# The attention out-projection as three fp16 products of high and low parts, in place of one fp32 product

## What is computed

```
x = queries                                    # (4, 1024, 128) fp32
q, k, v = split(layernorm(x) @ [Wq, Wkv])      # 16 heads of 64; q, k rotated in 32 of them
attn = softmax(q @ k.T * 64 ** -0.5)
out  = (attn @ v) of all heads side by side    # (4, 1024, 1024)
x = x + out @ Wout + bout                      # <- the out-projection; Wout is (1024, 128)
x = x + gelu(layernorm(x) @ U1 @ V1 + b1) @ U2 @ V2 + b2
```

## Time and profile before

| | |
|---|---|
| median of 3 runs | 1453.45 us (1453.07 to 1453.85) |
| the profiled execution's own time | 1453.33 us |
| its span, first to last instruction | 1451.5 us |
| granted TensorE clock, mean | 0.986 of full speed |
| PE busy | 1386.7 us (96%) |
| DVE busy | 1161.0 us (80%) |
| POOL busy | 989.8 us (68%) |
| ACT busy | 789.7 us (54%) |
| PE's 504 records of the out-projection in TILE | 66.7 us |

### The profile page before, as it was taken

The page is one execution under the profiler, slowest core; times in us unless marked ns, Lnnn a source line. Parts: engine busy times, 40 slices in busy tenths (PEclk is TensorE's granted clock), DMA queues, the critical chain, the costliest instruction groups (busy, mean ns, idle before and its releaser), DMA issues.

```text
span 1451.5 us, 25538 instructions
## 1 busy us (share of the span) xinstructions
PE 1386.7 (96%) x7313; PEld 518.3 (36%) x7313; DVE 1161.0 (80%) x1296; ACT 789.7 (54%) x1511; POOL 989.8 (68%) x499
## 2 busy tenths in 40 slices
PE   3698999999999999999999999999999999999897
PEld 1133333343434333333433333343433333343334
DVE  6786888888788888878888888878888887889644
ACT  3254555555555555646555555555555564655456
POOL 4379776858486677858677685848667784867831
PEclk9699999999999999999999999999999999999999
DMA  5402121220313122130312222031312213031002
GB/s 160 87 20 63 37 66 38 58 58 15 83 34 80 22 59 58 39 78 15 80 37 62 40 58 58 15 81 36 80 22 58 58 37 79 15 80 28 11 16 58
DMA packets 69553, 75.46 MB, mean 52 GB/s; under 512 B 26804, under 2 KB 36536, under 8 KB 69272
## 3 DMA queue, kind: packets, MB, share of 16 engines
q1 hardware_dynamic: 68080, 74.14, 22.8%
q10 hardware_dynamic: 1448, 1.00, 0.3%
HBM read 22.04 MB, written 2.35 MB: 17 GB/s over the span
## 4 chain that ended last, share of the span: by engine, by line
PE 48%; issue 23%; POOL 22%; DVE 4%; ACT 2%; POOLq 1%; DMA 0%; ACTq 0%; SPq 0%; DVEq 0%
PE O L389 17%; PE S L377 9%; POOL SA L677 9%; PE S L378 8%; PE M L398 5%; POOL T L653 5%; PE TILE L307 3%; PE TILE L331 3%; POOL STAGE L664 3%; POOL YR L656 2%; DVE MX L603 2%; ACT PF L512 1%; PE TILE L323 1%; PE TILE L313 1%; POOL WRAW L293 1%
## 5 line engine op out<-in xcount | busy, mean ns | idle before, releaser
L677 POOL TENSOR_TENSOR SA<-PF 128x1024 f32<-128x1024 f32 x254 | 658.7, 2601 | 364.8 <-DVE SUM L610 303.0
L512 ACT ACTIVATE PF<-S 128x512 f32<-128x512 f32 x1024 | 555.8, 596 | 456.7 <-PE S L378 455.1
L603 DVE TENSOR_REDUCE MX<-M 128x1 f32<-128x1024 f32 x508 | 597.3, 1217 | 179.4 <-PE M L398 179.2
L389 PE MATMUL O<-PF,V 128*64 128x512 f32 x2048 | 497.9, 607 | 0.0
L377 PE MATMUL S<-QK 128*128 128x512 f16 x1024 | 393.2, 384 | 4.6 <-ACT PF L512 3.2
L378 PE MATMUL S<-QK 128*128 128x512 f16 x1024 | 389.1, 380 | 0.0
L613 DVE TENSOR_TENSOR SUM<-SUM,SA 128x1024 f32<-128x1024 f32 x126 | 225.2, 1787 | 5.3 <-POOL SA L677 4.2
L389 PEld LDWEIGHTS O<-PF,V 128*64 128x64 f32 x2048 | 124.8, 136 | 249.9 <-issue 179.4
L377 PEld LDWEIGHTS S<-QK 128*128 128x128 f16 x1024 | 99.2, 97 | 250.7 <-ACT PF L512 107.9
L398 PE MATMUL M<-QK 64*128 64x512 f16 x1016 | 169.2, 410 | 16.2 <-DVE MX L603 8.5
L398 PEld LDWEIGHTS M<-QK 64*128 64x128 f16 x1016 | 53.2, 152 | 222.6 <-issue 210.1
(11 more groups left out here) (107 smaller groups left out, 750.6 us busy)
## 6 DMA issues: line engine op xcount, KB each, us to landing
QK<-STAGE SPq DMA_DIRECT2D x128, 256.0 KB, 3.9
QK<-STAGE SPq DMA_DIRECT2D x128, 128.0 KB, 3.1
RB<-den SPq DMA_DIRECT2D x124, 128.0 KB, 3.0
X<-in_L_attn_queries SPq DMA_DIRECT2D x4, 512.0 KB, 13.1
out<-X SPq DMA_DIRECT2D x8, 256.0 KB, 2.3
RT<-DS SPq DMA_DIRECT2D x124, 2.0 KB, 1.7
WRAW<-in_L_attn_Wkv SPq DMA_DIRECT2D x1, 1024.0 KB, 9.0
ROPE<-in_rope SPq DMA_DIRECT2D x1, 1024.0 KB, 12.3
```

The lines of the kernel that those rows point to most:

```text
L389: mm = e.matmul(O[DH * z:DH * z + DH, :], V[:, h, kt * DH:(kt + 1) * DH], PF[:, t % SLOTS, z * HALF:(z + 1) * HALF], start=(kt == 0), stop ...
L512: e.activation(PF[:, t % SLOTS, z * HALF:(z + 1) * HALF], S[:, z * HALF:(z + 1) * HALF], ACT.Exp, scale=EXP_SCALE).then_inc(exped, 1)
L603: e.tensor_reduce(MX[:, place % 2, q:q + 1], bank, AX, ALU.max).then_inc(max_read, 1)
L677: e.tensor_tensor(SA[:, (t // 2) % 2, :], PF[:, t % SLOTS, :], PF[:, t % SLOTS + 1, :], ALU.add).then_inc(two_summed, 1)
```

## The change

The product `OS @ WO` in fp32 becomes `OH @ WH + OL @ WH + OH @ WL` in fp16, accumulated in one PSUM group. `WH` is Wout times 16 rounded to fp16 and `WL` what is left; both are made once, ahead of the loop, by ACT and DVE from a raw copy of Wout that is now loaded into the last slot of `PF`. For each pair, `OH` is `OS` rounded to fp16, copied by ACT behind its work of steps 16 and 26 (`HIGH_AT`), and `OL` is `OS - OH`, made by DVE in steps 17 and 27 (`LOW_AT`). The residual add divides by 16. `OH` and `OL` have one buffer each, so ACT's copy waits until the pair before has been added.

```diff
+HIGH_AT = {16: 1, 26: 0}
+LOW_AT = {17: 1, 27: 0}
...
-        WO = sb("WO", [P, HEADS // 2, D], F32)
+        WO = sb("WO", [P, 2, HEADS // 2, D], F16)
...
+        OH = sb("OH", [P, 2, HALF], F16)
+        OL = sb("OL", [P, 2, HALF], F16)
...
+        WO_RAW = PF[:, SLOTS - 1, :].rearrange("p (c n) -> p c n", n=D)
...
         def out_tile(e, q, parity, pair, z, bank):
-            e.wait_ge(normed, q + 1)
+            e.wait_ge(out_lo, q + 1)
             for j in range(4):
-                mm = e.matmul(bank[:, j * P:(j + 1) * P], OS[:, parity, z, j * P:(j + 1) * P], WO[:, pair, :],
-                              start=True, stop=True)
+                tokens = slice(j * P, (j + 1) * P)
+                for n, (o, w) in enumerate(((OH, 0), (OL, 0), (OH, 1))):
+                    mm = e.matmul(bank[:, tokens], o[:, z, tokens], WO[:, w, pair, :], start=(n == 0), stop=(n == 2))
             mm.then_inc(tile_made, 1)
...
+        def act_out_high(e, q, parity):
+            e.wait_ge(normed, q + 1)
+            wait(e, added, 2 * q)
+            e.activation(OH[:, :, :], OS[:, parity, :, :], ACT.Copy).then_inc(out_hi, 1)
...
             act_tiles(e, it, t)
+            if t in HIGH_AT and not (it.first and HIGH_AT[t]):
+                act_out_high(e, it.pair(HIGH_AT[t]), HIGH_AT[t])
...
-            e.tensor_tensor(xs, bank.rearrange("p (t d) -> p t d", d=D), xs, ALU.add).then_inc(added, 1)
+            e.scalar_tensor_tensor(xs, bank.rearrange("p (t d) -> p t d", d=D), 1.0 / WSCALE, xs, ALU.mult,
+                                   ALU.add).then_inc(added, 1)
...
+        def dve_out_low(e, q, parity):
+            e.wait_ge(out_hi, q + 1)
+            e.tensor_tensor(OL[:, :, :], OS[:, parity, :, :], OH[:, :, :], ALU.subtract).then_inc(out_lo, 1)
...
             if it.last:
                 dve_last(e, t)
+            if t in LOW_AT and not (it.first and LOW_AT[t]):
+                dve_out_low(e, it.pair(LOW_AT[t]), LOW_AT[t])
...
+            act.wait_ge(wo_in, 16)
+            act.activation(WO[:, 0, :, :], WO_RAW, ACT.Copy, scale=WSCALE).then_inc(wo_hi, 1)
             act_max(act, 0, 0)
...
             for c in range(EARLY - 1):
+                if c == 1:
+                    act_out_high(act, PAIRS - 1, 1)
                 gelu(c + 1)
                 q_copy(c)
...
+            dve.wait_ge(wo_hi, 1)
+            dve.scalar_tensor_tensor(WO[:, 1, :, :], WO_RAW, WSCALE, WO[:, 0, :, :], ALU.mult,
+                                     ALU.subtract).then_inc(wo_lo, 1)
...
             norm.then_inc(normed, 1)
+            dve_out_low(dve, PAIRS - 1, 1)
```

More of the change, by code:

```diff
@@ L204, in build @@
         inverse_spread, stored = sem("inverse_spread"), sem("stored")
+        wo_hi, wo_lo, out_hi, out_lo = (sem(n) for n in ("wo_hi", "wo_lo", "out_hi", "out_lo"))
         powers_set = sem("powers_set")
@@ L777, in _ @@
                 sp.dma_start(X[:, b * KT:(b + 1) * KT, :], xr[:, b * KT:(b + 1) * KT, :]).then_inc(x_in[b], 16)
-            sp.dma_start(WO[:, :, :], wout_d.rearrange("(c p) n -> p c n", p=P)).then_inc(wo_in, 16)
+            sp.dma_start(WO_RAW, wout_d.rearrange("(c p) n -> p c n", p=P)).then_inc(wo_in, 16)
             sp.wait_ge(rot_lo, 4)
@@ L930, in body @@
                     if it.first and OUT_AT.get(t) == (0, 0):
-                        e.wait_ge(wo_in, 16)
+                        e.wait_ge(wo_lo, 1)
                     pe_step(e, it, t)
```

## The result

The changed kernel took 1459.09 us (median of 6 runs, 1456.73 to 1460.14), the kernel before 1452.79 (6 runs, 1452.22 to 1453.85): a ratio of 1.0040, 95% interval 1.0027 to 1.0053. So it is slower, by about 6 us, 0.4 us above the point forecast. The profiled execution took 1457.93 us over a span of 1456.1, 4.6 more than the span before. So the medians differ by 6.3 us and the two traced executions by 4.6, where +5.4 was forecast; all that follows by stages is read from these two executions.

The account below looks back on a forecast made before the run. PE, busy 96% of the span, was taken to bound the kernel; on 1453.33 us, -0.8 (middle) + 0.8 + 0.9 (first) + 2.9 (last) + 1.6 (behind the loop) = +5.4 gave 1458.7 us, range 1446 to 1465.

Parts of the forecast that it names:

- The tile: Out-projection tile on PE: twelve fp16 products take 0.67 us instead of 0.89 for fp32, 0.22 less for each of 64.
- ACT's copy: OH copy of 1.04 us ahead of step 17's exponentials, hidden with 1.7 us to spare; the same in step 26.
- Who goes first: Steps 17 to 20, middle iteration: POOL's waiting pair sum precedes DVE's sum of step 17; PE 0.60 us late at step 20.
- DVE keeps its turn: Rival: POOL's wait ends only when DVE issues something else; middle iterations gain 0.58 each, total 1447.3 us; chance 0.12.
- the stalls don't come: Rival: OL is shorter or doesn't exclude POOL; 62 tiles gain 0.22, the tail costs 1.6, total 1441.3 us; chance 0.08.
- Middle iterations: 14 iterations: +0.60 stall less 0.66 from three tiles, -0.06 each, -0.8 us in all.
- First iteration: OL delays the turned tile of step 29: +0.8 us net, plus +0.9 for a stretch at the lower clock.
- +1.0: First iteration: OL delays the residual add of step 28 and step 29's turned tile by about 1.0 us.
- +0.9 for one such stretch: First iteration: PE at the lower clock behind its grown gap of some 3 us, +0.9 us, bounds 0 and twice that.
- Last iteration: Down tile of step 19 +2.3, steps 26 to 28 +1.2, less 0.22 for three tiles each: +2.9 us.
- Behind the loop: PE's last out-projection tiles wait for OL, +2.1, less 2 x 0.22 for shorter tiles: +1.6 us.
- the rival on the lower clock: Gaps in the last iteration and after the loop bring lower clock, 0.9 us each: 1460.5, up to 1462.3; chance 0.15.

Follow-up runs that it names:

- e2_no_low: Changed kernel with DVE's difference OL left out everywhere, the tile reading OH in its place; 1441.87 us, ratio 0.9922 to the kernel before.
- e4_reduce: Changed kernel with OL made by a one-operand tensor_reduce in place of the two-operand subtraction; 1443.30 us, ratio 0.9935 to the kernel before.
- e5_step21: Changed kernel with parity 1's OL in step 21, tiles in steps 22 and 23, except in the last iteration; 1463.65 us, ratio 1.0088 to the kernel before.
- even schedule: Changed kernel, middle iterations: v tile of step 24 in step 18, parity 1's OL in step 21, its tiles in 22 and 24; 1446.47 us, ratio 0.9961.

## Why the prediction was right, step by step

- *The tile* at 0.67 and *ACT's copy* hidden: right, by the rows after and the kernels without OL and with the fp32 tile.
- *Who goes first*: right. POOL's waiting pair sum went ahead of DVE's next instruction; the sum of step 17 took 3.38 where about 3.4 followed. "DVE keeps its turn" and "the stalls don't come" both fall.
- *Middle iterations*: forecast -0.06 each, measured -0.12; over the 14, from +4.1 to +2.6 above, -1.5 and not -0.8. The kernel without OL shows both parts: 82.99 less 0.85 for the tiles, and 0.74 given back.
- *First iteration*: "+1.0" for the gap was right: the turned tile is 1.49 later, of which 0.46 was there by step 20 (den tile at 111.57 and 112.03; the clock of 57 to 70 us was 0.83 and not 0.86, 13 x 0.03 = 0.4, before any new work of the loop). "+0.9 for one such stretch" was mis-sized. From the turned tile to the tile of step 30 PE took 150.80 - 144.04 = 6.76 us where it took 146.46 - 142.55 = 3.91: 2.85. I had priced the stretch by PE's busy time around the earlier gap, where PE was idle for 2.78 of 6 us; behind this one PE had dense work at 1.2 GHz. The kernel with the turned tile moved ran without it. That the growth of the gap brings the stretch, as I assumed, is not shown: the same place cost 1.62 behind a gap of 1.78 (without OL), and nothing behind 1.83 (OL in step 21).
- *Last iteration*: this step failed. I expected +2.9; from 2.59 late at step 6 to 2.80 behind the loop it was +0.2. The down tile of step 19 did wait for the residual add, 1.57, and steps 26 to 28 gave +1.28 where 1.2 was forecast. But PE had come 1.64 closer ahead of it (V tile of step 16: 1366.50 before, 1367.45 after, +0.95), since in the kernel before 1360 to 1364 was at a clock of 0.62 and here at 1.00, and the eight value matmuls of step 16 took 3.11 there and 1.94 here. DVE's normalise had not come closer (1364.48, 1366.60: +2.12), and the residual add ended +2.20: OL itself made it only 0.1 later. One reason is DVE's idle 0.92 ahead of the maxima, which the sum's lateness ate first; the other is that OL and POOL's line 693 were issued 0.01 us apart and OL went first, so the sum waited for one short instruction and not for a pair sum. PE's value matmuls, the stretch and DVE's maxima of step 18, before and then after:

```profile
1362.00 3.11 PE L389 MATMUL O<-PF,V 128*64 128x512 f32 x8
1360.00:1364.00 4.00, 3.01 (x10) 1.48 (x12) 1.26 (x2) 0.60 (x1) 2.07 (x2) 0.62 0.00 0
1371.15 2.35 DVE L603 TENSOR_REDUCE MX<-M 128x1 f32<-128x1024 f32 x2 [0.92 <-PE M L398]
...
1364.12 1.94 PE L396 MATMUL O<-PF,V 128*64 128x512 f32 x8
1360.00:1364.00 4.00, 2.04 (x14) 1.02 (x12) 2.15 (x3) 2.41 (x5) 3.84 (x5) 1.00 0.00 0
1373.35 2.34 DVE L619 TENSOR_REDUCE MX<-M 128x1 f32<-128x1024 f32 x2
```

- *Behind the loop*: +2.1 for the wait was right (1417.45 to 1422.37 is +4.92, less 2.80). That the whole came to +1.8, near the +1.6, is luck. The wait was followed by matmuls at the lower clock, which the rival on the lower clock had named: PE's first tile of line 997 (970 before) is 6.06 late (1421.20 and 1427.26), which is 1.58 more than 2.80 + 2.12 - 0.44. And the kernel before ran its own last matmuls slowly, the changed kernel did not, which gave 1.46 back. The last matmuls of lines 951 and 978, before and after:

```profile
1444.20 1.94 PE L951 MATMUL S<-QK,U 128*32 128x512 f32 x8
...
1449.66 1.06 PE L978 MATMUL S<-QK,U 128*32 128x512 f32 x8
```

So the sum hit 1458.7 against 1459.1 partly by luck: the first iteration was 2.4 more than forecast (0.46 of it the clock's start), the last 2.7 less, the middle ones 0.7 less, the end 0.2 more: 5.4 + 2.4 - 2.7 - 0.7 + 0.2 is the 4.6 of the spans. The sign and the mechanism of the middle iterations are shown by experiment, and so are the waits in the first iteration and behind the loop; for the last iteration I have read the trace only. Where PE's clock falls from run to run stays open, and with it the size of every term outside the middle iterations.

## What to carry to other kernels

Before putting a DVE instruction with two SBUF operands into a tuned schedule, look for a place where POOL stands idle too, and follow whom POOL's lateness reaches: here it was DVE's own next sum, or ACT's queue and the next transfers. When a PE tile is moved, ask which latency it covered where it stood. Price a PE gap not by its own length alone: the matmuls behind it may run at the lower clock, and whether they do differed here from trace to trace.

## What was not expected of the hardware

- Behind an idle gap of 2.88 us PE took 2.85 more for what followed, at the lower level; in the kernel without that gap it ran at 1.00. Gaps of 1.78 to 1.89 us at this place were followed by the lower level in two traces (e2_no_low, e4_reduce) and by full speed in two (before, e5_step21).
- Kernels differ in their spread from run to run: 1.0 us over 5 runs for the even schedule, 7.7 over 4 for the fp32 tile with OL.
- Of two excluding instructions issued within 0.01 us of each other, DVE's went first (one meeting); of one that waits and one that is issued as its predecessor ends, the waiting one did, at every such meeting shown above.
